# Scores by key in four row groups of 32 partitions, and one turn for the maxima of all heads

## The reference

```python
x = x + jnp.tanh(g_xattn[0]) * _L0_xattn_ref(_layernorm(x), ctx_1024, ...)   # 16 heads of 16, scale 1/sqrt(16)
x = x + jnp.tanh(g_ffn[0])   * _L0_ffn_ref(_layernorm(x), ...)               # FFT, product, inverse FFT: one real 256x256 product
x = x + jnp.tanh(g_xattn[1]) * _L1_xattn_ref(_layernorm(x), ctx_1024, ...)   # 16 heads, relative position bias, no scale
x = x + jnp.tanh(g_ffn[1])   * _L1_ffn_ref(_layernorm(x), ...)               # 8 experts, 2 for each token, squared relu, 512 hidden
```

## Time and profile before

| what | value |
|---|---|
| median of three runs | 2374.21 us |
| profiled execution | 2374.52 us, span 2372.7 us |
| busy | PE 1969.1 us (83%), PEld 1749.7 (74%), DVE 1319.2 (56%), ACT 748.8 (32%), POOL 957.8 (40%) |
| chain that ended last, by engine | PE 47%, DMA 20%, issue 12%, DVE 8%, POOL 6%, ACT 5% |
| mean granted clock of TensorE | 0.952 of 2.4 GHz |
| 500 to 1000 us | PE busy 447.96 of 500, DVE 327.76, ACT 147.32, POOL 229.12, clock 0.98 |

### The profile page before, as it was taken

How to read it: one execution, slowest core, us unless ns; L and a number is a source line. 1 busy time by engine, 2 the same in 40 slices (tenths; PEclk the granted TensorE clock), 3 DMA queues, 4 the chain that set the end, 5 groups by cost and what they waited for, 6 DMA issues and landing times.

```text
span 2372.7 us, 44105 instructions
## 1 busy us (share of the span) xinstructions
PE 1969.1 (83%) x13970; PEld 1749.7 (74%) x14003; DVE 1319.2 (56%) x3668; ACT 748.8 (32%) x1509; POOL 957.8 (40%) x1332
## 2 busy tenths in 40 slices
PE   2798988989889898898988989888079888888884
PEld 1687877878778788788888878877067677677663
DVE  2466666666666666666666676665544333333331
ACT  2223323233232322323223233232244444444432
POOL 0344445344453444534444444442323333333333
PEclk7799999999999999999999999999589999999997
DMA  5000101000010100100001000010443333333332
GB/s 116 12 10 30 29 9 38 9 29 29 9 38 9 29 29 9 38 9 29 29 9 38 9 29 29 9 35 6 154 93 60 58 58 58 58 58 58 58 49 29
DMA packets 93909, 88.58 MB, mean 37 GB/s; under 512 B 26904, under 2 KB 87320, under 8 KB 93880
## 3 DMA queue, kind: packets, MB, share of 16 engines
q0 software_dynamic: 26160, 35.87, 8.8%
q1 hardware_dynamic: 67720, 52.33, 8.1%
HBM read 43.77 MB, written 44.39 MB: 37 GB/s over the span
## 4 chain that ended last, share of the span: by engine, by line
PE 47%; DMA 20%; issue 12%; DVE 8%; POOL 6%; ACT 5%; SPq 1%; POOLq 1%; DVEq 0%; ACTq 0%
PE scores L1088 25%; DMA out<-y,ids 19%; PE bank L1088 18%; POOL sorted_rows L667 3%; PE bank L1156 3%; DVE t_lo L893 1%; ACT routed L781 1%; DVE biased L970 1%; POOL rstd L614 1%; ACT t_hi L746 1%; DVE e L967 1%; ACT q_hi L751 1%; PE scores L1213 1%; POOL kb_hi L632 1%; ACT neg_mx L756 1%
## 5 line engine op out<-in xcount | busy, mean ns | idle before, releaser
L695 POOL DMA_INDIRECT out<-y,ids x136 | 211.8, 1557 | 461.3 <-ACT y L805 281.1
L614 POOL TENSOR_TENSOR rstd<-var,half_power 128x2 f32<-128x2 f32 x128 | 90.2, 705 | 568.6 <-DVE var L880 567.9
L1088 PE MATMUL scores<-vb,pr 128*128 128x136 f32 x2048 | 280.3, 279 | 0.7 <-ACT pr_rest L767 0.7
L1088 PEld LDWEIGHTS scores<-vb,pr 128*128 128x128 f32 x2048 | 256.9, 190 | 5.9 <-ACT pr_rest L767 4.1
L943 DVE TENSOR_REDUCE mx<-scores 128x8 f32<-128x512 f32 x256 | 169.6, 684 | 139.3 <-remote 81.5
L1072 DVE SCALAR_TENSOR_TENSOR h<-scores,relu 128x512 f32<-128x512 f32 x136 | 94.1, 692 | 272.6 <-ACT relu L799 266.7
L1088 PE MATMUL scores<-q_hi,kb_hi 128*128 128x256 f32 (+1 forms) x640 | 197.7, 309 | 34.5 <-ACT neg_mx L756 34.5
L746 ACT ACTIVATE t_hi<-bank 128x512 fp32r<-128x512 f32 x192 | 114.8, 598 | 346.3 <-PE bank L1156 346.1
L893 DVE TENSOR_TENSOR t_lo<-bank,t_hi 128x512 fp32r<-128x512 f32 x192 | 132.1, 688 | 120.8 <-ACT t_hi L746 117.9
L667 POOL DMA_INDIRECT sorted_rows<-routed,place x128 | 126.8, 990 | 169.2 <-ACT routed L781 138.1
L1088 PE MATMUL scores<-up_hi,xt_hi 128*128 x272 | 120.6, 443 | 84.5 <-DVE xt_lo L1066 84.3
(11 more groups left out here) (222 smaller groups left out, 5746.8 us busy)
## 6 DMA issues: line engine op xcount, KB each, us to landing
xe<-sorted_rows SPq DMA_DIRECT2D x136, 128.5 KB, 2.1
x<-x_rows SPq DMA_DIRECT2D x32, 256.0 KB, 2.9
out<-x_end SPq DMA_DIRECT2D x32, 256.0 KB, 3.0
raw<-w_up_t SPq DMA_DIRECT2D x8, 512.0 KB, 4.3
raw<-w_down_t SPq DMA_DIRECT2D x8, 512.0 KB, 4.6
ctx<-ctx_t SPq DMA_DIRECT2D x32, 77.0 KB, 2.7
out<-y,ids POOLq DMA_INDIRECT x136, 3.8
sorted_rows<-routed,place POOLq DMA_INDIRECT x128
```

Of the source, the lines that this page charges most:

```text
L614: pool.tensor_tensor(rstd[u][:], var[u][:], half_power[:], ALU.pow).then_inc(sem(f"rstd_ready{u}"), 1)
L695: pool.indirect_dma_start(out=acc, out_offset=bass.IndirectOffsetOnAxis(ap=ids[j][:], axis=0), in_=y[j][:], in_offset=None, compute_op=ALU ...
L1088: last = pe.matmul(dst, w, m, start=n == 0, stop=n == len(pairs) - 1)
```

## The change

Five things, all in part 1:

1. `by_key` for the main tiles: tile j takes 32 partitions alone (j*32 to j*32+31, the features of its two heads; the other partitions of these columns are zero). The four tiles go in turn, round by round: first kb_hi x q_hi of tiles 0 to 3, then kb_lo x q_hi, kb_hi x q_lo, `expand` x `neg_mx`. Each tile writes a bank of its own (bank j, columns g*256 on). At layer 1 the 16 bias matmuls, over all partitions, come first. One semaphore increment follows both groups.
2. `expand` has its ones in rows 32*(h//2) + h%2, and `mx` gets 32 columns for each pair of heads (zero but for two), so that a turned block has each head's maximum in that row.
3. `turn_max` is one step: four full transposes to bank 4 and one copy of 128x512.
4. The order in `half`: one turn, key scores of both groups, exp 0, slot 5, exp 1, rest tile, slot 6, exp 2, slot 7. Before, the turn of group 1 lay between key scores, slot 5 between the two groups, slot 6 ahead of exp 1 and the rest tile.
5. `kb_hi` and `kb_lo` have one copy for both layers; `pr` is ordered by tile, then group.

```diff
-        expand[h, h * S0:(h + 1) * S0] = 1
-        expand[h, MAIN + h * S1:MAIN + (h + 1) * S1] = 1
+        row = 2 * DH * (h // 2) + h % 2
+        expand[row, h * S0:(h + 1) * S0] = 1
+        expand[row, MAIN + h * S1:MAIN + (h + 1) * S1] = 1
...
-        kb_hi = sb1("kb_hi", [P, 2, 2, G, KEYS], F32R)
+        kb_hi = sb1("kb_hi", [P, 2, G, KEYS], F32R)
...
-        mx = [sb1(f"mx{u}", [P, NC, H]) for u in range(2)]
+        mx = [sb1(f"mx{u}", [P, NC, G, NJ, 2 * DH]) for u in range(2)]
...
-            do["turn_max"](*a, 0)
+            do["turn_max"](*a)
             fill(4)
-            do["by_key"](*a, 0, range(0, 2))
-            do["turn_max"](*a, 1)
-            do["by_key"](*a, 0, range(2, NJ))
+            do["by_key"](*a, 0)
+            do["by_key"](*a, 1)
             do["exp"](*a, 0)
             fill(5)
-            do["by_key"](*a, 1, range(NJ))
+            do["exp"](*a, 1)
+            do["by_key"](*a, 2)
             fill(6)
-            do["exp"](*a, 1)
-            do["by_key"](*a, 2, ())
             do["exp"](*a, 2)
             fill(7)
...
-                    wait(pool, f"sc_done{u}", num(t, 2 * (G + 1), (l - 1) * (G + 1)))
+                    wait(pool, f"sc_done{u}", num(t, 4, l * 2))
...
+            def turn_max(u, t, l):
+                act.wait_ge(sem(f"mt_done{u}"), num(t, 2, l + 1))
+                act.activation(neg_mx[u][:].rearrange("p g t -> p (g t)"), sc[:, 4, :], ACT.Copy, scale=-1.0).then_inc(sem(f"neg_mx_ready{u}"), 1)
...
-                act.wait_ge(sem(f"sc_done{u}"), num(t, 2 * (G + 1), l * (G + 1) + g + 1))
+                act.wait_ge(sem(f"sc_done{u}"), num(t, 4, l * 2 + g // G + 1))
...
+            def turn_max(u, t, l):
+                pe.wait_ge(sem(f"mx_ready{u}"), num(t, 2 * G, l * G + G))
+                for g in range(G):
+                    for c in range(NC):
+                        last = pe.transpose(sc[:, 4, g * T + c * P:g * T + (c + 1) * P], mx[u][:, c, g].rearrange("p i r -> p (i r)"), ident[:])
                 last.then_inc(sem(f"mt_done{u}"), 1)
...
+            def by_key(u, t, l, g):
+
+                if g == 0:
+                    pe.wait_ge(sem(f"neg_mx_ready{u}"), num(t, 2, l + 1))
                 if g < G:
                     pe.wait_ge(sem(f"q_lo_ready{u}"), num(t, 2 * G, l * G + g + 1))
+                if l == 1 and g == 0:
+                    for j in range(NJ):
+                        for gg in range(G):
+                            for b_ in (bias_hi, bias_lo):
+                                pe.matmul(sc[:, j, gg * T:(gg + 1) * T], ident_r[:], b_[:, gg, j], start=gg == 0 and b_ is bias_hi, stop=False)
+                if g < G:
+                    for n in range(4):
+                        for j in range(NJ):
+                            rows, keys = slice(j * 2 * DH, (j + 1) * 2 * DH), slice(j * P, (j + 1) * P)
+                            k_, q_ = ((kb_hi[rows, u, g, keys], q_hi[u][rows, g]), (kb_lo[rows, u, g, keys], q_hi[u][rows, g]),
+                                      (kb_hi[rows, u, g, keys], q_lo[u][rows, g]), (expand[rows, keys], neg_mx[u][rows, g]))[n]
+                            last = pe.matmul(sc[:, j, g * T:(g + 1) * T], k_, q_, start=l == 0 and g == 0 and n == 0, stop=g == G - 1 and n == 3)
+                    if g == G - 1:
+                        last.then_inc(sem(f"sc_done{u}"), 1)
```

More of the change, by code:

```diff
@@ L172, in build @@
         v_tmp = sb1("v_tmp", [REST, D])
-        mx = [sb1(f"mx{u}", [P, NC, H]) for u in range(2)]
+        mx = [sb1(f"mx{u}", [P, NC, G, NJ, 2 * DH]) for u in range(2)]
         mx_rest = sb1("mx_rest", [P, NC, H])
         neg_mx = [sb1(f"neg_mx{u}", [P, G, T], F32R) for u in range(2)]
-        pr = [sb1(f"pr{u}", [P, G, NJ, T]) for u in range(2)]
+        pr = [sb1(f"pr{u}", [P, NJ, G, T]) for u in range(2)]
         pr_rest = [sb1(f"pr_rest{u}", [REST, G, T]) for u in range(2)]
@@ L269, in cols @@
         def cols(t, l, u, g, tile):
-            return t[:, l, u, g, tile * P:tile * P + (P if tile < NJ else REST)]
+            return t[:, u, g, tile * P:tile * P + (P if tile < NJ else REST)]
         def carrier(engine):
@@ L566, in _ @@
             for u in range(2):
-                pool.memset(neg_mx[u][:].bitcast(F32), 0.0).then_inc(sem("consts"), 1)
+                pool.memset(mx[u][:], 0.0).then_inc(sem("consts"), 1)
             pool.iota(iota_e[:], pattern=[[1, E]], base=0, channel_multiplier=0,
@@ L950, in join_max @@
                 dve.wait_ge(sem(f"m_read{u}"), num(t, 10, l * 5 + (3, 5)[g]))
-                heads = slice(g * HG, (g + 1) * HG)
-                dve.tensor_tensor(mx[u][:, :, heads], mx[u][:, :, heads], mx_rest[:, :, heads], ALU.max).then_inc(sem(f"mx_ready{u}"), 1)
+                heads = mx[u][:, :, g, :, 0:2]
+                rest = mx_rest[:, :, g * HG:(g + 1) * HG].rearrange("p c (i e) -> p c i e", i=NJ)
+                dve.tensor_tensor(heads, heads, rest, ALU.max).then_inc(sem(f"mx_ready{u}"), 1)
             def sums(u, t, l, c, g):
@@ L1203, in by_token @@
                     dst, cut = (sc[:, NC * g + c], slice(0, MAIN)) if n != 2 else (sc[:, 4, b * REST:(b + 1) * REST], slice(MAIN, KEYS))
-                    pairs = [(q_hi[u][:, g, c * P:(c + 1) * P], kb_hi[:, l, u, g, cut])]
+                    pairs = [(q_hi[u][:, g, c * P:(c + 1) * P], kb_hi[:, u, g, cut])]
                     if l == 1:
@@ L1214, in turn_max @@
                 last.then_inc(sem(f"mt_done{u}"), 1)
-            def by_key(u, t, l, g, tiles):
+            def by_key(u, t, l, g):
+                if g == 0:
+                    pe.wait_ge(sem(f"neg_mx_ready{u}"), num(t, 2, l + 1))
                 if g < G:
-                    pe.wait_ge(sem(f"neg_mx_ready{u}"), num(t, 2 * G, l * G + g + 1))
                     pe.wait_ge(sem(f"q_lo_ready{u}"), num(t, 2 * G, l * G + g + 1))
[L1221 to L1229, removed]
+                if l == 1 and g == 0:
[12 more added lines that the diff above has]
+                        last.then_inc(sem(f"sc_done{u}"), 1)
+                else:
+                    for gg in range(G):
+                        pairs = [(k_, q_[:, gg]) for k_, q_ in passes(cols(kb_hi, l, u, gg, NJ), cols(kb_lo, l, u, gg, NJ), q_hi[u], q_lo[u])]
+                        pairs.append((expand[:, MAIN:KEYS], neg_mx[u][:, gg]))
+                        if l == 1:
+                            pairs += [(ident_r[0:REST, 0:REST], b_[0:REST, gg, NJ]) for b_ in (bias_hi, bias_lo)]
+                        last = product(sc[0:REST, 4, gg * T:(gg + 1) * T], pairs)
@@ L1238, in sums @@
                 first = ((l * 2 + u) * G + g) * NJ * GV
-                pairs = [(pr[u][:, g, j, part], vflat[:, first + j * GV:first + (j + 1) * GV]) for j in range(NJ)]
+                pairs = [(pr[u][:, j, g, part], vflat[:, first + j * GV:first + (j + 1) * GV]) for j in range(NJ)]
                 pairs.append((pr_rest[u][:, g, part], vr[:, l, u, g].rearrange("p h v -> p (h v)")))
```

25 lines of the change are left out of this document (9 added, 16 removed).

## The result

| | before | after |
|---|---|---|
| median, us (7 runs each) | 2372.85 (2369.73 to 2375.39) | 2396.87 (2382.10 to 2407.93) |
| profiled execution, us | 2374.52 | 2396.87 |

Ratio 1.0105, 95% interval 1.007 to 1.014. I forecast 2364 us; rival 2 gave 2397. The runs of the changed kernel are also wider apart (1.1% against 0.24%), and their times follow the mean granted clock: 2382.1 us at 0.930, 2396.9 at 0.923, 2407.9 at 0.918.

A forecast was written before the change was run, and what follows sets the result against it. TensorE, busy for 83% of the span and 47% of the chain, was taken as the bound. 2374.5 - 22 (halves) + 11 (clock) = 2364 us; 8-in-10 range 2332 to 2440, likeliest case 2350 to 2385.

The forecast's parts named there:

- rival 2: Clock falls in the new waits: first and third halves each pay 1.4 us every pass, 2397 us; chance 0.15.
- Rounds: Key scores by row groups: 8 rounds of four matmuls at 0.16 us, 1.3 us in place of 3.75 per half.
- Rival 1: Weight loads of four row groups go one after the other, a round takes 0.45 us: 2480 us; chance 0.12.
- Going in and out: Switching TensorE into row groups and back: 0.1 us each way, 0.2 per half.
- Late start: Key scores wait for one turn of the maxima: about 2 us later in first and second halves, 555.2 against 554.93 in fourth.
- Second half tied to POOL: Second half: xn still waits for POOL's scatter and rstd, so the 2 us saved there gain 0.
- Third half: Late key scores and t_hi behind the second exp delay the feed-forward product, 539.1 against 537.72: loss 1.4 us.
- Fourth half: Sums start at 563.25, not 565.69: gain 2.4 us, with gate, DVE routing chain and hot_sum wait moving along.
- First half: Rest of the values waits for DVE copies behind POOL's scatters, 587.1 against 587.53: gain 0.4 us.
- The sum: The four halves together: 0 - 1.4 + 2.4 + 0.4 = 1.4 us a pass, 22 us in 16 passes.
- The clock: Granted clock falls after new TensorE waits: half a fall a pass charged, 0.7 us, 11 us in all.
- Rival 3: Rounds of 0.12 us, no price for the switch, full clock: 2.4 us a pass, 2336 us; chance 0.15.

The follow-up runs named there:

- e10: Changed kernel with unread products in its new TensorE waits and 5 ahead of the wait for hot_sum: 2348.3 us, ratio 0.9876.
- e2: Kernel before, with 7 unread products ahead of its wait for hot_sum in first and fourth halves: 2356.0 us, ratio 0.9911.
- e3: Changed kernel, but in the third half alone slot 6 (turn, t_hi) comes ahead of the second exp: 2365.5 us, ratio 0.9955.
- e1: Changed kernel with unread products put into its new waits on TensorE, none ahead of hot_sum: 2361.8 us, ratio 0.9936.
- e5: Changed kernel with unread products in its new waits and 7 ahead of the wait for hot_sum: 2356.1 us, ratio 0.9913.
- e9: Mended order of e7 plus unread products in the waits left, 7 of them ahead of hot_sum: 2295.2 us, ratio 0.9655.
- e8: Changed kernel with the four products of a tile one after the other, then the next tile: 2429.5 us, ratio 1.0228.
- e7: Changed kernel with mended order (products not needing neg_mx first, third half's turn and t_hi before second exp), no unread products: 2323.9 us, ratio 0.9785.
- e4: Changed kernel with key scores of the main tiles through all 128 partitions, same order: 2552.6 us, ratio 1.0748.
- e13: Mended order of e7 plus unread products in all waits left, 5 of them ahead of hot_sum: 2283.9 us, ratio 0.9635.

## Why the prediction was wrong

Point by point, by its own steps:

- *Rounds*: right in kind, 0.12 us in place of the 0.16 taken, all four side by side. Rival 1 (loads in turn) is out.
- *Going in and out*: 0.2 per half taken; 0.3 measured, with the late second round. The cheaper rounds pay for it.
- *Late start*: token scores to key scores 6.3, 6.3, 6.6 and 6.8 us in first, second, third and fourth halves (e10), against 4.3, 4.3, 4.9 and 6.5 in e2; I had 2, 2, 1.6 and 0.3 more. Right.
- *Second half tied to POOL*: right, 22.35 us against 22.36.
- *Third half*: loss 1.4 forecast, 1.40 measured, 0.9 of it by ACT's order (e3).
- *Fourth half*: at the start of the sums the gain is 2.37 us (2.4 forecast); at the end of the half 1.85. Half a microsecond is lost on the way to `hot_sum`. I took it that the routing chain on DVE would only move. In the trace its first step after the gate took 0.59 us before and takes 1.06 after, where it begins with a copy of keys on POOL; after, and then before:

```profile
571.02 1.05 POOL L631 TENSOR_TENSOR kb_lo<-k_lo,head_of_dim 128x512 fp32r<-128x512 f32 x1
571.04 1.06 DVE L967 TENSOR_SCALAR e<-es 128x16 f32<-128x16 f32 x1 [0.70 <-ACT es L771]
```

```profile
569.02 1.04 POOL L632 TENSOR_TENSOR kb_lo<-k_lo,head_of_dim 128x512 fp32r<-128x512 f32 x1
569.50 0.59 DVE L967 TENSOR_SCALAR e<-es 128x16 f32<-128x16 f32 x1 [0.73 <-ACT es L772]
```

  DVE's step ends 0.03 us after POOL's in both pairs, wherever it began: with POOL first, DVE doesn't get on until POOL is through. Where no POOL instruction runs beside it, the same step takes 0.17 or 0.18 us (twice in each trace). The Trainium skill ("SBUF — State Buffer", "SBUF: two separate sides") has the rule: an instruction of one of the two can hold their shared ports until it ends, and the other waits. The trace agrees (1.06 against 0.59 us, and 0.17 alone); I didn't test it by moving POOL's copy.
- *First half*: 0.4 forecast, 0.3 measured.
- *The sum* of these was to be 22 us; it measured 7.8 (e10 against e2) to 12 (by halves). Most of what is missing is the fourth half's half microsecond.
- *The clock*: the step that failed. I charged half a fall a pass at 1.4 us, 11 us in all. There are 31 more falls, two a pass, and 123 us more at half clock: at 0.24 each 30 us, and by the table at e10 53.8 - 21.2 = 33 us. 2373 - 8 to 12 + 30 = 2391 to 2395, against 2397.

It is the count that was wrong, by four. My ground for half a fall was one wait of 1.71 us without and one of 2.08 with a fall, "as such waits end today with and without a fall". For a single wait that was near the truth: 35 of the 80 waits that are new or now longer end in one. But a pass has five of them (the turn in three halves, `xn` and `t_lo` in the second, `t_lo` in the third), not one, and I charged the half once. Half a fall at each of the five would have been 2.5 a pass; 2.2 were measured, and 0.25 fewer behind `hot_sum`. The trace before holds the rate as well, 23 falls in 32 waits for `hot_sum`, where I had looked at two.

The price of 1.4 us was right in third halves (1.5) and behind the turn in first halves (1.3). In second halves I had the falls hide behind POOL; they cost 10 us in all. Behind `hot_sum` one costs 0.9 us in the kernel before (21.2 us for 23), so that the average is 0.8 to 0.9.

The rivals: rival 2 named the mechanism, falls in the new waits. Its time, 2397, is luck: it has 45 us for the falls where they cost 33, in first and third halves alone where second halves pay too, and a gain of 22 where the change has 8 to 12, and the two errors cancel. Rival 3 (no price for the clock, 2336) is what e10 puts to the test: without falls the changed kernel takes 2348 us, and the kernel before, without its own, 2356.

## What to carry to other kernels

Row groups of 32 partitions were worth their full factor here (a round of 0.12 us in place of 0.47), where an operand is block-diagonal, but the kernel only gains when the work before and behind them keeps up: put first what doesn't need the late operand (here three of four products and the bias), and check on every other queue what the new order puts behind what. Then price each new wait of TensorE twice: its length, and the slow stretch after it. Count the waits, not the halves or the passes, and look which engine the stretch behind each wait holds up. A few products that nobody reads, placed in a wait that is there anyway, win back that second part; they cost nothing in e1 and e2, but in e5 and e9 two more of them came with the late exp, so try two counts; measure any change of a schedule once with them, so that its own effect is seen apart from the clock's.

## What the runs showed of the hardware that I had not expected

- A product on one group of 32 partitions is recorded as starting beside products on other groups that stand up to 12 matmuls earlier in the program (e8: four first products between 605.41 and 605.46 us).
- The exp that waits for the last key score can start 1.2 to 2.2 us after the recorded end of that matmul (an end that the profile models), in first and second halves (those in which POOL scatters): e5 1.6, e8 1.2, e7 and e9 2.2 us; 0.1 in the changed kernel, e1, e3, e4 and e10 to e13. Two unread products fewer in a far-away wait make it go. It costs 0.6 us in the second half. In all four kernels that have it the exp starts 1.0 to 1.1 us after the end of POOL's fourth scatter, however long the delay (medians 1.07, 1.02, 1.01 and 1.05 us); in e10 it starts 0.4 us before that end. So what is held up seems to come free with the scatters. Why it is held up in these four kernels and not in the others, whether by the code's position or otherwise, is open.
- A microsecond at half clock cost 0.24 us here on average, not 0.5: 0.45 in third halves, where TensorE is what the others wait for, and 0.15 in second halves, where POOL's chain covers most of it.
- A wait of TensorE of one and the same kind and length ends now with a fall, now without: 23 of 32 waits for `hot_sum` before (1.7 to 2.1 us), 20 of 48 at the turn of the maxima after (2.4 to 2.7 us, four turns included).
